# A two-layer transformer kernel: the query exponentials of layer 0 turned by VectorE blocks and a scratch round trip, for seven of eight batches

## The reference

```
xn = _ln(x) ; q = softmax(xn @ Wq + bq, over the 64 channels of a head)
k = softmax(xn @ Wk + bk + mask, over the 512 tokens)
v = (xn @ Wv + bv) * src_mask
att = einsum('bnhd,bnhl->bhdl', k, v)
y   = einsum('bnhd,bhdl->bnhl', q, att)
x   = x + silu(_ln(y) * (1 + scale) + shift) @ W_out + b_out
```

## Time and profile before

| | us |
|---|---|
| median of three executions | 1331.49 (1328.41 to 1332.4) |
| the profiled execution, its own time | 1329.64 |
| its span | 1327.8 |
| PE busy | 1285.4 (97%) |
| DVE busy | 987.1 (74%) |
| ACT busy | 912.9 (69%) |
| POOL busy | 491.2 (37%) |

### The profile page before, as it was taken

How to read it: one execution, slowest core, us unless ns; L and a number is a source line. 1 busy time by engine, 2 the same in 40 slices (tenths; PEclk the granted TensorE clock), 3 DMA queues, 4 the chain that set the end, 5 groups by cost and what they waited for, 6 DMA issues and landing times.

```text
span 1327.8 us, 25194 instructions
## 1 busy us (share of the span) xinstructions
PE 1285.4 (97%) x9480; PEld 1025.2 (77%) x9480; DVE 987.1 (74%) x1987; ACT 912.9 (69%) x2063; POOL 491.2 (37%) x451
## 2 busy tenths in 40 slices
PE   8999999999999999899999999999999999999998
PEld 6688888888788887577788788788788788788666
DVE  6678777776877867766876876976876877877766
ACT  5243433344343547888898898898898898898984
POOL 0527455374644470102512522522522512522502
PEclk9989999999999999889899999999999899999989
DMA  9231321404122365765464464464564464464422
GB/s 324 84 120 33 119 96 57 132 20 150 51 101 88 104 191 176 235 179 154 144 181 145 154 180 139 164 179 145 160 172 146 148 185 146 149 182 142 133 76 81
DMA packets 86122, 184.79 MB, mean 139 GB/s; under 512 B 7584, under 2 KB 8664, under 8 KB 85104
## 3 DMA queue, kind: packets, MB, share of 16 engines
q1 hardware_dynamic: 86000, 183.18, 44.4%
HBM read 115.46 MB, written 67.17 MB: 138 GB/s over the span
## 4 chain that ended last, share of the span: by engine, by line
PE 67%; DVE 13%; ACT 10%; POOL 5%; issue 2%; DMA 2%; SPq 0%; DVEq 0%; POOLq 0%; ACTq 0%
PE ps L544 13%; PE ps L546 13%; PE ps L545 12%; PE ps L723 8%; PE ps L697 6%; PE ps L705 6%; ACT ps L895 5%; PE ps L539 5%; DVE cT L1165 2%; ACT Pb L905 2%; PE ps L648 2%; DVE xr L1035 2%; PE ps L630 2%; DVE xTl L1039 2%; DVE st L1017 2%
## 5 line engine op out<-in xcount | busy, mean ns | idle before, releaser
L895 ACT ACTIVATE ps<-ps,cT 128x512 f32<-128x512 f32 x512 | 347.9, 722 | 19.2 <-DVE cT L1165 18.9
L1165 DVE TENSOR_REDUCE cT<-ps 128x1 f32<-128x512 f32 x512 | 320.6, 683 | 43.7 <-PE ps L697 42.0
L905 ACT ACTIVATE Pb<-ps 128x512 f32<-128x512 f32 x512 | 268.6, 660 | 44.5 <-PE ps L705 42.4
L697 PE MATMUL ps<-Ks,Qs 98*128 98x512 f32 x512 | 184.8, 425 | 18.5 <-ACT ps L895 17.0
L705 PE MATMUL ps<-Qs,Ks 100*128 100x512 f32 x512 | 159.0, 407 | 1.4 <-DMA Qs<-nxT 0.7
L697 PEld LDWEIGHTS ps<-Ks,Qs 98*128 98x128 f32 x512 | 96.7, 192 | 70.0 <-ACT ps L895 42.6
L895 ACT ACTIVATION_READ_ACCUMULATOR ps<-ps,cT 128x1 f32 x512 | 137.2, 268 | 0.0
L705 PEld LDWEIGHTS ps<-Qs,Ks 100*128 100x128 f32 x512 | 95.7, 189 | 38.0 <-ACT Pb L905 12.4
L544 PE MATMUL ps<-xTh,Wh_k 128*128 128x512 f32 x256 | 108.2, 423 | 10.4 <-DVE xTl L1039 7.4
L544 PE MATMUL ps<-Wh_o,sTh 128*128 128x512 f32 x256 | 102.2, 399 | 2.5 <-DVE sTl L1142 1.7
L544 PE MATMUL ps<-Wh_v,xTh 128*128 128x512 f32 x256 | 103.5, 404 | 0.0
(11 more groups left out here) (171 smaller groups left out, 2864.3 us busy)
## 6 DMA issues: line engine op xcount, KB each, us to landing
Qs<-stack_scratch SPq DMA_DIRECT2D x32, 768.0 KB
Ks<-stack_scratch SPq DMA_DIRECT2D x32, 768.0 KB
stack_scratch<-sg_q SPq DMA_DIRECT2D x32, 512.0 KB, 2.7
stack_scratch<-sg_k SPq DMA_DIRECT2D x32, 512.0 KB, 2.6
wr<-in_x SPq DMA_DIRECT2D x32, 256.0 KB, 5.8
x_scratch<-wr SPq DMA_DIRECT2D x32, 256.0 KB, 3.7
stack_scratch<-sg_q SPq DMA_DIRECT2D x32, 256.0 KB, 2.9
stack_scratch<-sg_k SPq DMA_DIRECT2D x32, 256.0 KB, 3.1
```

The lines of the kernel that those rows point to most:

```text
L697: e.matmul(bank[:], Qs[par][0:RX, j, t * 128:(t + 1) * 128], Ks[par][0:RX, j, :], start=True, stop=True).then_inc(s["S"], 1)
L895: e.activation(bank[:], bank[:], ACT.Exp, bias=nx[:, n % 2, j, t, 0:1], accum_out=dn[:, b % 2, t, 4 * g + j:4 * g + j + 1]).then_inc(s["S_ ...
L905: e.activation(Pb[m][:, j, :], ps[bank_of["a", n, m, j]][:], ACT.Exp).then_inc(s["P"], 1)
L1165: e.tensor_reduce(nx[:, n % 2, j, t, 0:1], ps[bank_of["S", n, j, t]][:], AX.X, ALU.max, negate=True).then_inc(s["S_max"], 1)
```

## The change

For batches 0 to 6 `eq` is kept in blocks of 32 channels (`blocks`). After `qn`, four DVE transposes of 32 x 32 blocks (`qt`) turn them in place; four transfers of 256 KB write them to a DRAM scratch in runs of 512 bytes, and one transfer of 1 MB reads them back as `qT` (`qio`). The 16 PE transposes `tq` and the four ACT copies of such a batch are gone; batch 7 keeps them. `qT` is now one buffer of four chunks. The key scale `krc` moves from those copies into `sta`, which moves from ACT to DVE; the copies of y out of PSUM move from DVE to ACT. The tokens of y of these batches come out in another order, so the loads and stores of `wr` use rows in that order (`rows`). The order of layer 0 is written anew: `te` now stands in the `q` section, `y` of batch b in the `q` section of batch b+1, `ty` of batch b at the end of `k` and the start of `v` of batch b+2, and `o` of batch b behind `q` of batch b+2, where it was behind `q` of batch b+1. In layer 1, s of batches 8 to 14 gets a place of its own (`sTf`) in place of `yb`.

```diff
+LAG = (0, 1, 2, 2.5, 3, 3.5, 4, 5, 5.5, 6, 7, 2, 3, 8)
...
+        if b >= 2:
+            L0.append((tiles("o", b - 2), at + 3, at + 4))
+        L0.append((tiles("te", b), *lag(1)))
...
+            L0.append((tiles("qt", b), *lag(4)))
+            L0.append(([("qio", b)], *lag(5)))
+            L0.append(([("y", b, g) for g in range(5)], *lag(6)))
...
     if k == "y" and i == 0:
-        return ([("tq", p[1], p[2])],) * 2 if p[2] < NC else ([], [])
+        return ([("tq", p[1], p[2])],) * 2 if p[2] < NC and not by_scratch(p[1]) else ([], [])
...
+            def qt(i, b, t):
+                e.wait_ge(s["q_nrm"], 4 * b + t + 1)
+                e.transpose(blocks(eq, b)[:, :, t, :], blocks(eq, b)[:, :, t, :]).then_inc(s["q_bt"], 1)
...
+                if i == 0:
+                    e.wait_ge(turned, 4 * n + 4)
+                    if n:
+                        e.wait_ge(back, 16 * n)
+                    blocked = src[:].rearrange("p t d -> p (t d)").rearrange("p (c n) -> p c n", n=128)
+                    for a in range(4):
+                        e.dma_start(scratch.rearrange("(c i) n -> i c n", i=32)[:, :, 128 * a:128 * a + 128],
+                                    blocked[32 * a:32 * a + 32]).then_inc(out, 16)
+                else:
+                    e.wait_ge(out, 64 * (n + 1))
+                    if free:
+                        e.wait_ge(*free)
+                    e.dma_start(dst, scratch.rearrange("(c p) n -> p c n", p=128)).then_inc(back, 16)
```

More of the change, by code:

```diff
@@ L129, in the_order @@
     first_m = [("m", 0, 0, 0), ("m", 0, 0, 1)], [("m", 0, 1, 0), ("m", 0, 1, 1)]
+    L0 = []
     for b in range(B):
[L131 to L145, removed]
@@ L146, in the_order, with lag @@
-        if not last:
[L147 to L150, removed]
+        first, last, at = b == 0, b + 1 == B, 4 * b
+        def lag(i):
+            lo, hi = PLAN["0x"][i]
+            return at + LAG[i] + 2 * lo, at + LAG[i] + 2 * hi
@@ L369, in cond_two_layers @@
         eq = sb("eq", [128, NT, D], c=c0)
[L370 removed]
+        qT = sb("qT", [128, NC, T], c=c0)
         A0 = sb("A0", [128, NC, 128], c=c0)
@@ L440, in s_tile, with turned, u_tile @@
             ch, t, n = half(x, c)
-            return tok(x, ps[bank_of["ty", x, c]][:, 0:n.stop - n.start]) if in_bank(x) else yb[:, t, ch * 128:(ch + 1) * 128]
+            return tok(x, ps[bank_of["ty", x, c]][:, 0:n.stop - n.start]) if s_in_bank(x) else tok(x, sTf[:, c, :])
+        def turned(x, c):
+            return 4 * x + c + 1
+        def u_tile(x, c):
+            ch, _, n = half(x, c)
+            return ps[bank_of["ty", x, c]][:, 0:n.stop - n.start]
         def done(key):
@@ L634, in y @@
             def y(i, b, g):
-                if i == 0 and g < NC:
+                if i == 0 and g < NC and not by_scratch(b):
                     bank = take(("tq", b, g))
@@ L825, in q @@
                     if t == 0 and b:
-                        e.wait_ge(s["q_tr"], 4 * b)
+                        e.wait_ge(s["q_out"], 64 * b)
                     e.wait_ge(s["q_sub"], 4 * b + t + 1)
[L828 to L839, removed]
+                    e.activation(blocks(eq, b)[:, :, t, :], vt[t % 2][:].rearrange("p (c i) -> p c i", i=32), ACT.Exp).then_inc(s["q_exp"], 1)
             def y(i, b, g):
[L842 to L845, removed]
+                if i == 0 and g < NC and not by_scratch(b):
                     if g == 0:
[L847 to L850, removed]
+                        e.wait_ge(s["y_mm"], 4 * b)
+                    e.wait_ge(s["q_tr"], g + 1)
+                    e.copy(qT[:, g, :], ps[bank_of["tq", b, g]][:]).then_inc(s["q_T"], 1)
+                if i == 1 and g:
+                    g -= 1
+                    if g == 0:
+                        e.wait_ge(*((s["yn_tr"], 4 * b) if b else (s["em"], 4)))
+                    e.wait_ge(s["y_mm"], 4 * b + g + 1)
+                    e.copy(natural(yb)[:, 4 * g:4 * g + 4].rearrange("p c t i -> p t c i"),
+                           ps[bank_of["ym", b, g]][:].rearrange("p (t c i) -> p t c i", t=NT, i=32)).then_inc(s["y_sc"], 1)
             def ty(i, x, c):
```

142 lines of the change are left out of this document (102 added, 40 removed), and 2 rows, old and new, of the table PLAN.

## The result

The changed kernel takes 1346.2 us in the median (1344.2 to 1348.4, four executions), beside 1330.7 for the kernel before (1328.4 to 1332.4): a ratio of 1.0117, 95% interval 1.0097 to 1.0137. It is slower, by 15.5 us, and lies above the predicted range. The page of the profiled execution, which answers to the earlier trace rows: busy time of each engine, then the granted clock in 40 slices of 33.6 us.

What follows compares the result with a forecast made beforehand. The prediction took layer 0 to be bound by the columns PE streams. Its terms, -12.8 + 8.0 + 2.3 - 0.8 - 1.6 + 2.5 = -2.4, gave a median of 1329.1 us, range 1319 to 1341 (8 in 10).

Steps and rivals of the forecast that it cites:

- scratch trip: Exponentials written to DRAM and read back: write 7 us, read 5.5, hidden with 4 us to spare; late-trip rival 0.08.
- transition: Layer 0 to layer 1: PE waits for the last `eq`, behind POOL's multiplies; +2.5 us (0 to 5).
- plain batches: Layer 0's ordinary batches: `xTl` about as tight as before, +0.5; with the slow batch's 2.1 not recurring, -1.6 us together.
- layer 1: Keeps its order, and PE did not wait on POOL's `yb` there: 0.
- count of transposes: PE work removed: seven batches lose four groups of transposes each, 28 x 0.46 = -12.8 us.
- `xn` late: Rival: POOL's `xn` chain makes PE wait 3 us in each of six batches, +18, 1340 to 1347; chance 0.15.
- About as tight as today: Plain batches: last `xTl` ends 16 to 17 us behind `q`, `k` asks at 16.5; +0.5 over all.
- second batch: Without `o` behind its `q`, PE waits for `xTl`: stall 8.3 us, +8.0 net, and +2.3 for half clock behind it.
- The one that ended on the slower side: The same rival as `xn` late: 1340 to 1347, chance 0.15.

Runs made afterwards that it cites:

- e1: The changed kernel with the `wr` row transfers of batches 0 to 6 back on 128 consecutive rows (output not the reference's); 1334.0 us, ratio 1.0034.
- f1: The kernel before with only the new row order added, four groups of 32 rows for batches 0 to 6; 1336.4 us, ratio 1.0051.
- k1: The changed kernel with plain row transfers, tokens put back in order by the instructions that write `sTh` and `sTl`; output correct; 1334.8 us, ratio 1.0032.
- k4: k1 with the sums, reciprocals and multiplies of batch 7's exponentials placed earlier; 1336.5 us.
- k7: k1 with the transposes and casts of layer 1's first tokens (batch 8) placed inside `o` of batch 5; 1335.1 us.
- k9: k1 with the moves of both k4 and k7; 1333.4 us.
- g3: The changed kernel with the row transfers of batches 0 to 6 over 16 groups of 8 rows instead of four of 32; 1335.7 us.
- h1: e1 without the scratch writes of the turned exponentials, `qT` read from an input instead; 1333.9 us.

## Why the prediction was wrong

**The step that failed is one that isn't there.** The part on the scratch trip costs the new transfers, `q_scratch` and `qT`, and the part on the transition costs POOL's multiplies. Nowhere is there a term for the 56 row transfers of `wr` whose address pattern the change rewrites. The diff keeps their number, bytes and run length of 2 KB, and I took them for unchanged. Their outermost dimension went from 128 rows to four groups, and their rate from up to 379 GB/s to 102. Worth: 12 us (e1 against the changed kernel), 6 us in the kernel before (f1). The remaining 6 us of the 18.2 are terms that were there and came out too small: 2.1 in the transition and 3.3 in the plain batches, taken apart below, and 0.8 in layer 1, which was put at 0 and was not looked into.

**The transition** was forecast at +2.5. Its mechanism was there and its wait is about that of the forecast, 2.7 us for `eq`. Yet without the slow transfers the stretch still costs 2.8 + 1.8 (the four groups of transposes it saves) = 4.6. In k1, PE's timeline from the end of `o` of batch 5 to the first `q` product of layer 1 reads:

```profile
461.67 1.91 PE L608 MATMUL ps<-identr,xin 128*128 128x128 f32 x16
466.25 0.63 PE L608 MATMUL ps<-identr,eq 128*128 128x128 f32 x4 [2.67 <-POOL eq L1398]
466.71 1.47 PE L608 MATMUL ps<-identr,yb 128*128 128x128 f32 x12
468.02 0.60 PE L608 MATMUL ps<-identr,eq 128*128 128x128 f32 x4
468.46 0.60 PE L608 MATMUL ps<-identr,yb 128*128 128x128 f32 x4
469.01 1.13 PE L720 MATMUL ps<-A,qT 128*128 128x128 f32 x8
469.97 0.60 PE L608 MATMUL ps<-identr,eq 128*128 128x128 f32 x4
472.49 0.47 PE L613 MATMUL ps<-xTh,Wh_q 128*128 128x512 f32 x1 [1.91 <-issue]
```

No product in 10.8 us. Before, the 16 transposes of `xin` stood in four groups between the products of an `o`, which ended at 473.0, and the casts ran under it:

```profile
460.91 0.60 PE L539 MATMUL ps<-identr,xin 128*128 128x128 f32 x4
462.75 0.60 PE L539 MATMUL ps<-identr,xin 128*128 128x128 f32 x4
```

The other two groups start at 464.57 and 467.10. I had costed the one wait I could name (`eq`) and not asked what else becomes late when the cover is gone: k4, k7 and k9 show three inputs late at the same place, `eq`, the operand of batch 8 and the last part of Wq, each hidden by the next. How much each is worth by itself they don't show, since no version came clear of k1.

**The plain batches** were to be 55.2 us long and are 56.2, against 57.0 in the earlier trace rows:

```profile
232.40:288.60 56.20, 54.78 (x290) 46.27 (x289) 44.09 (x92) 19.63 (x36) 30.79 (x29) 1.00 0.38 127
288.60:344.80 56.20, 54.73 (x290) 46.23 (x289) 44.09 (x92) 19.61 (x36) 30.78 (x29) 1.00 0.38 127
```

PE's work fell by 1.9 us a batch, as the count of transposes had it (4 x 0.46 = 1.84), and one wait for `xTl` a batch, mostly of 1.4 us, came. That is the rival "`xn` late", at half its size: the last `xTl` comes 1.4 us after `k` asks, where I had put it level. "About as tight as today" was a comparison of two numbers near 16.5, one of which the prediction gives only as 16 to 17.

**The second batch.** Forecast: stall 8.3, half clock 2.3. The windows:

```profile
110.00:115.00 5.00, 0.94 (x3) 0.49 (x3) 2.04 (x2) 1.14 (x2) 4.92 (x6) 0.99 0.00 0
115.00:120.00 5.00, 2.05 (x4) 1.24 (x5) 3.63 (x6) 1.24 (x2) 2.80 (x2) 0.50 0.00 0
120.00:125.00 5.00, 4.68 (x11) 3.19 (x11) 4.52 (x12) 0.62 (x1) 2.52 (x3) 0.50 0.33 113
```

PE is idle 4.06 + 2.95 + 0.32 = 7.3 us, and 10 us run at a clock of 0.50, 1.2 GHz. While PE waits the clock costs nothing: of the 10 us it is busy 6.7, so 3.4 us are lost. The mechanism was right, and the sum, 7.3 + 3.4 = 10.7 against 10.6, is so close partly by luck: the stall came out 1.0 shorter and the clock's loss 1.1 larger. The prediction read that loss, 2.3, from the window of the earlier trace rows, but windows of 1 us show the kernel before at 0.50 from about 67.6 to 74.4, nearly 7 us, of which PE was busy 6.3: a loss of 3.2. The clock had fallen by 115, while PE stood, and was full again in the window from 125.

**The trip** was right in what counts, no wait, and near in its parts. I took 7 us for the whole write; from the issue of the first of its four transfers to that of the read, which waits for all of them, it is 6.9 to 11.0 us (5.5 is the median of one quarter). The read took 5.4, the block transposes 0.684 us where I took 0.7. The new form of `qn` costs POOL 1.05 us, where I allowed for up to double the 1.24 of the old.

**The rivals.** The one that ended on the slower side forecast 1340 to 1347 and would have been called right by the time alone; the trace refutes it at that size (five waits of 1.4 to 1.8 us, not six of 3).

## What to carry to other kernels

A transfer whose address pattern a change rewrites is a new transfer, even where bytes and run length stay: read its outermost dimension, find the share of DMA engines that it can use, and price it and what queues behind it. Where tokens must be permuted, let an instruction do it that writes them anyway, at no cost here, and keep the transfers plain. And where a change takes away the product that covered a stretch, list every input that was made under it, not only the one that is waited for first.

## What the runs showed of the hardware

- A transfer from SP over G groups of rows kept G of 16 DMA engines busy: G = 2, share 0.13 and 51 GB/s; G = 4, 0.26 and 102; 128 rows, up to 1.02 and 379 (with the end of another load in the window). That is 24 to 25 GB/s an engine. Sixteen scattered groups were as fast as plain rows (g3, 1335.7 us; e1, 1334.0).
- The Trainium skill has the rule, which the prediction didn't use: in "DMA: Bandwidth & Descriptors", section "Why a DMA increments its semaphore by 16 and not by 1", a transfer runs on the largest number of engines up to 16 that divides the slowest dimension of both sides. The traces agree for 2, 4 and 128; for 16 the time does, and a share of 1.00 in g3.
- Other transfers on the same queue were held up too: 7.6 us to landing in the median against 2.8, and in the last 4 us before the latest of them landed the share was 0.26 and 0.24. That a load over all 16 must wait for its share on the four busy ones fits this, but no view shows single engines, so it is argued and not shown.
- Writes of 512-byte runs, 256 KB each, landed in 5.5 us (4.6 with plain rows), and leaving them out gained nothing beyond the 2 us of the interval (h1 against e1).
- Behind waits of 6.9 us (changed kernel, batch 7) and 5.4 us (k7), and in the stall of the second batch, PE's granted clock fell to 0.50 and stayed there for several us of work: 1.6 us lost in the first, 3.4 in the last.
